# Dense attention on one Trainium2 core: value products of two key tiles in one go, with four sets of probabilities

## The chip, the cores and the metric

The kernel is one program on one core of a Trainium2 chip. The metric is the device time of a whole execution in microseconds (us); of several runs the median is given.

## What is computed

The reference is a chain of eight blocks on x of 2 x 512 rows of 256: four attentions, each followed by a feed-forward block. Two parts of it are plain softmax attentions of 16 heads of 16, and these two are what the change is about:

```
# part 6 of the program ("l3"): x attends to a context of 1024 rows, per batch
logit = jnp.einsum('bhnd,bhmd->bhnm', q, k)          # q already scaled
attn  = jax.nn.softmax(logit, axis=-1)
out   = jnp.einsum('bhnm,bhmd->bhnd', attn, v)

# part 5 ("m2"): x attends to its own 512 rows
scores = jnp.einsum('bqhd,bkhd->bhqk', q, k) * scale
probs  = jax.nn.softmax(scores, axis=-1)
out    = jnp.einsum('bhqk,bkhd->bqhd', probs, v)
```

All other blocks are left as they are.

## The kernel before, in words

`dense_attention` (from line 803) is called once for m2, with 512 keys, and once for l3, with 1024. It works through G = 8 groups (2 batches x 4 groups of heads) of S = 4 heads each, with 512 queries. The keys of a group are cut into tiles of 128: NC_ = 4 tiles in m2, 8 in l3. Each group needs two passes over the scores:

- **First pass** (`first_pair`, matmul at L893): queries on the partitions, keys along the free axis, two banks of PSUM (1024 scores a row) at a time. VectorE reduces such a pair to row maxima (`row_maxima`, L976, tile `shift`). There are two such pairs of banks, and pair k is written only after pair k-2 has been reduced (semaphore `pair_used`). The maxima of a group are transposed (`turn`, L900), negated and cut into two parts by VectorE (`cut`, L985 and L987), and put by two DMAs (L853) into two rows of the augmented queries `qa`, so that the second scores come out already shifted. A group has 8 pairs in m2 and 16 in l3.
- **Second pass** (`second`, L909): keys on the partitions, one matmul for each head of a tile, in three PSUM banks used in turn (semaphore `exp_done`: matmul i waits for exponential i-3). ScalarE takes the exponential (L1037) into `probs` in SBUF. `value_products(n, t)` (L919) then multiplies the probabilities of tile t of group n by the values: four matmuls, one for each head, on four column strips of 32 of the array, accumulated over the tiles in one bank (VALUES). They are float32, and the trace shows each as two records. A column "of v" holds a one, so that the denominators come out with them. Behind the last tile ScalarE copies the bank to `o_all` (L1040).

TensorE's order is written out by hand at the end of the tensor block. For each tile it is: pair, two seconds, pair, two seconds; behind them, from the second tile of a group, the value products of the tile before. First pairs run ahead of the second pass by one group and LEAD = 4 pairs (EARLY), so in tile t of group n the first pairs are of group n+1 and, from t = 2 in m2 (t = 6 in l3), of group n+2; the last 6 tiles of m2 and the last 10 of l3 have none left. `turn(n + 1)` stands behind the scores of tile NC_ - 2.

The operands of a group come through three buffers (BUFS). SyncE issues `load_qk(n - 1 + BUFS)`, four DMAs at L664 and L667, and `load_v` (L673) when the value products of group n-1 are done (`pv_done`). GpSimd clears two rows of the same buffer (L874) at the same point. `first_pair` with k = 0 waits for these loads (`qk_loaded`).

In the last group, `denominators` (L930) and `spread_pair` (L940) are put between the tiles; VectorE makes the reciprocals for them.

Of the kernel before, what the change touches and what calls it, by code (L numbers as in the profile page):

```python
# [9 lines left out]
ACT = mybir.ActivationFunctionType  # L10
AX = mybir.AxisListType

P = 128
# [3 lines left out]
NQ = 512  # L17
# [785 lines left out]
def dense_attention(nc, name, ps, ident, slot_pick, spread, nk, tiles, o_all):  # L803


    G, S, BUFS, LOADS = 8, 4, tiles.BUFS, tiles.LOADS
    NC_ = nk // P
# [11 lines left out]
    def pair_place(i):  # L819

        return i + max(0, (i - 2) // PAIRS)

    def turn_place(n):

        return (n + 1) * PAIRS + 2 + n if n < G - 1 else ALL + n

    LAST = ALL + G
    with Stage(nc, name) as s:
# [1 line left out]
        qk_loaded, v_loaded = tiles.qk_loaded, tiles.v_loaded  # L830
        shift = s.sb("shift", [P, 2, ROWS])
        minus_hi, minus_lo = s.sb("minus_hi", [ROWS, P], F32R), s.sb("minus_lo", [ROWS, P], F32R)
        probs = s.sb("probs", [P, 2 * S, NQ])
        rden = s.sb("rden", [P, NQ])
        rden_parts = s.sb("rden_parts", [P, NQ], F32R)
        zeroed = s.sem("zeroed")
# [3 lines left out]
        scored, exp_done, pv_done = s.sem("scored"), s.sem("exp_done"), s.sem("pv_done")  # L840
# [5 lines left out]
        @block.sync  # L846
        def _(sp):
            def place(n):
                sp.wait_ge(lo_ready, n + 1)
                if n >= BUFS:  # L850
                    sp.wait_ge(shift_cleared, n - BUFS + 1)
                for part, src in enumerate((minus_hi, minus_lo)):
                    sp.dma_start(qa[64 + part:65 + part, n % BUFS, :, :].rearrange("o h (t n) -> o (h t) n", n=P  # L853
                                                                                   ).bitcast(F32),
                                 src[:, :].bitcast(F32)).then_inc(shift_placed, 16)

            tiles.finish_first(sp)
            place(0)
            for n in range(G - 1):
                if n > 0:  # L860
                    sp.wait_ge(pv_done, NC_ * n)
                    if n - 1 + BUFS < G:
                        tiles.load_qk(sp, n - 1 + BUFS)
                    tiles.load_v(sp, n + 1)
                place(n + 1)
# [10 lines left out]
        @block.tensor  # L876
        def _(pe):
            def first_pair(i):
                n, k = divmod(i, PAIRS)
                buf = n % BUFS  # L880
                if k == 0:
                    pe.wait_ge(qk_loaded[buf], LOADS * (n // BUFS + 1))
                    if n < BUFS:
                        pe.wait_ge(filled, 2 * n + 2)
                    else:
                        pe.wait_ge(shift_cleared, n - BUFS + 1)
                at = pair_place(i)
                if at >= 2:
                    pe.wait_ge(pair_used, at - 1)
                for half in range(2):  # L890
                    r, j = divmod(2 * k + half, NH)
                    h, t = divmod(r, QT)
                    ins = nc.tensor.matmul(ps[:, 2 * (at % 2) + half, :], qa[:, buf, h, t * P:(t + 1) * P],  # L893
                                           ka[:, buf, h, j * BANK:(j + 1) * BANK], start=True, stop=True)
                ins.then_inc(pair_made, 1)

            def turn(n):
                at = turn_place(n)
                pe.wait_ge(pair_used, max(at - 1, pair_place((n + 1) * PAIRS - 1) + 1))
                nc.tensor.transpose(ps[0:ROWS, 2 * (at % 2), 0:P], shift[:, n % 2, :], ident[:, :]  # L900
                                    ).then_inc(shift_turned, 1)

            def second(n, t, h):
                i, buf = (n * NC_ + t) * S + h, n % BUFS
                if t == 0 and h == 0:
                    pe.wait_ge(shift_placed, 32 * n + 32)
                if i >= 3:
                    pe.wait_ge(exp_done, i - 2)
                nc.tensor.matmul(ps[:, 4 + i % 3, :], ka[:, buf, h, t * P:(t + 1) * P], qa[:, buf, h, :],  # L909
                                 start=True, stop=True).then_inc(scored, 1)  # L910

            def value_products(n, t):
                pe.wait_ge(exp_done, (n * NC_ + t) * S + S)
                if t == 0:
                    pe.wait_ge(v_loaded[n % 2], 16 * (n // 2 + 1))
                if t == 0 and n > 0:
                    pe.wait_ge(o_copied, n)
                for h in range(S):
                    ins = nc.tensor.matmul(ps[32 * h:32 * h + 32, VALUES, :], v[:, n % 2, t, h, :],  # L919
                                           probs[:, t % 2 * S + h, :], start=(t == 0), stop=(t == NC_ - 1))  # L920
                ins.then_inc(pv_done, 1)

            def denominators(half):
                begin, end = HALVES[half]
                m, at = 4 * (end - begin), LAST + 4 * half
                pe.wait_ge(o_copied, end)
                pe.wait_ge(pair_used, at - 1)
                for n in range(begin, end):
                    pick = 28 - 4 * (n - begin)
                    ins = nc.tensor.matmul(ps[64:64 + m, 2 * (at % 2), :], slot_pick[:, pick:pick + m], o_all[:, n, :],  # L930
                                           start=(n == begin), stop=(n == end - 1))
                ins.then_inc(den_made, 1)

            def spread_pair(i):
                half = 0 if i < 3 else 1
                at = LAST + 1 + half + i
                pe.wait_ge(rden_lo, half + 1)
                pe.wait_ge(pair_used, at - 1)
                for j in range(2):
                    ins = nc.tensor.matmul(ps[:, 2 * (at % 2) + j, :], spread[64:128, 2 * i + j - HALVES[half][0], :],  # L940
                                           rden_parts[64:128, :], start=True, stop=True)
                ins.then_inc(pair_made, 1)

            for i in range(PAIRS + 2):
                first_pair(i)
            turn(0)
            for i in range(PAIRS + 2, EARLY):
                first_pair(i)
            for n in range(G):
                for t in range(NC_):  # L950
                    for h in range(S):
                        i = EARLY + 2 * (n * NC_ + t) + h // 2
                        if h % 2 == 0 and i < ALL:
                            first_pair(i)
                        second(n, t, h)
                    if t == TURN_AT and n < G - 1:
                        turn(n + 1)
                    if n == G - 1 and t == 0:
                        denominators(0)
                    if n == G - 1 and 1 <= t <= 3:  # L960
                        spread_pair(t - 1)
                    if t > 0:
                        value_products(n, t - 1)
                value_products(n, NC_ - 1)
            denominators(1)
            spread_pair(3)
# [61 lines left out]
        @block.scalar  # L1028
        def _(act):
            for n in range(G):  # L1030
                for t in range(NC_):
                    for h in range(S):
                        i = (n * NC_ + t) * S + h
                        act.wait_ge(scored, i + 1)
                        if i >= 2 * S:
                            act.wait_ge(pv_done, n * NC_ + t - 1)
                        nc.scalar.activation(probs[:, t % 2 * S + h, :], ps[:, 4 + i % 3, :], ACT.Exp  # L1037
                                             ).then_inc(exp_done, 1)
                act.wait_ge(pv_done, n * NC_ + NC_)
                nc.scalar.activation(o_all[:, n, :], ps[:, VALUES, :], ACT.Copy).then_inc(o_copied, 1)  # L1040
# [1990 lines left out]
```

## Time and profile before

| | |
|---|---|
| time, median of 3 runs | 3491.04 us (3489.39 to 3491.08) |
| the profiled execution's own time | 3486.16 us |
| its span | 3484.4 us |
| TensorE busy in the span | 2558.5 us (73%) |
| VectorE busy | 2113.5 us (61%) |
| ScalarE busy | 1431.6 us (41%) |
| mean granted TensorE clock | 0.845 of full speed |
| second pass of m2, from the first L909 to the last | 2506.1 to 2631.0 us |
| second pass of l3, the same | 3029.2 to 3233.4 us |

"Busy" is the share of the span in which an engine has a computing instruction in flight. A matmul's record lasts longer than the time it keeps the next one from starting, so the distance of two starts tells more than a duration. The two attentions of the change take about a tenth of the span together. A timeline merges like instructions that follow each other: "0.73 PE L893 ... x2" is two matmuls, from the start of the first to the end of the last.

### The profile page before, as it was taken

What the parts mean: (1) busy time and instruction counts of PE and PEld (TensorE: products, weight loads), DVE (VectorE), ACT (ScalarE), POOL (GpSimd) and SP (SyncE); (2) the same over time, 40 slices, a digit from 0 to 9 for tenths busy, and PEclk for the clock granted to TensorE, in tenths of its full rate; (3) what the DMA queues carried; (4) which work ended last, traced back from release to release, by engine and by line L of the source; (5) the groups of instructions that cost most, each with busy time, mean ns of one, the idle gap of its engine ahead of it and who ended that gap; (6) DMA issues with size and microseconds to landing.
All of it is one profiled execution on the core that took longest, in us unless ns stands there. A gap on an engine that the chain in (4) does not pass through costs nothing. (4 is left out here: it accounts for less than half of the span.)

```text
span 3484.4 us, 37704 instructions
## 1 busy us (share of the span) xinstructions
PE 2558.5 (73%) x12065; PEld 1618.6 (46%) x12066; DVE 2113.5 (61%) x4913; ACT 1431.6 (41%) x2245; POOL 423.8 (12%) x228
## 2 busy tenths in 40 slices
PE   2999999536366666665499459788785896899598
PEld 1444444324233333333499435455443775454387
DVE  4667666575777777753366435665654565676377
ACT  1444444111677887773244122221251231266221
POOL 0000000002000000000477302111100211100021
PEclk8999999767677777776699779999797997899799
DMA  1000000206011111000366200000420110631010
GB/s 57 14 14 9 14 14 0 87 5 209 9 25 25 25 25 25 7 1 8 120 205 201 79 28 1 0 0 0 141 65 23 42 42 14 187 89 41 29 41 30
DMA packets 72294, 170.09 MB, mean 49 GB/s; under 512 B 10185, under 2 KB 38865, under 8 KB 68689
## 3 DMA queue, kind: packets, MB, share of 16 engines
q1 hardware_dynamic: 70608, 164.11, 15.9%
q0 software_dynamic: 1536, 4.20, 0.4%
q8 instruction: 68, 1.11, 0.1%
q14 instruction: 82, 0.66, 0.1%
HBM read 129.09 MB, written 38.80 MB: 48 GB/s over the span
## 5 line engine op out<-in xcount | busy, mean ns | idle before, releaser
L1449 ACT ACTIVATE l1a_over_s<-l1a_sc_s,l1a_minus_step_s 128x1024 bf16<-128x1024 f32 x256 | 290.0, 1139 | 3.5 <-DVE l1a_minus_step_s L1323 2.2
L1263 DVE MAX8 l1a_cand_s<-ps 128x8 f32<-128x128 f32 x1024 | 213.2, 284 | 70.5 <-PE ps L1158 67.2
L1191 PE MATMUL ps<-l1a_probs_s,l1h_v_s 128*32 128x256 f32 x1024 | 124.3, 574 | 158.6 <-ACT l1a_probs_s L1457 157.4
L1435 ACT ACTIVATE l1a_sc_s<-ps,l1a_minus_tau_s 128x1024 f32<-128x1024 f32 x128 | 141.9, 1112 | 139.6 <-DVE l1a_minus_tau_s L1292 53.4
L976 DVE TENSOR_REDUCE l3a_shift_s<-ps 128x1 f32<-128x1024 f32 x128 | 150.2, 1219 | 50.6 <-PE ps L893 50.6
L538 DVE TENSOR_SCALAR l0a_probs_s<-l0a_probs_s 128x1024 f32<-128x1024 f32 x128 | 88.5, 691 | 150.5 <-ACT l0a_probs_s L605 150.0
L605 ACT ACTIVATE l0a_probs_s<-ps 128x1024 f32<-128x1024 f32 x128 | 131.1, 1024 | 104.5 <-PE ps L455 103.3
L1158 PE MATMUL ps<-l1h_ka_s,l1h_qa_s 128*128 128x512 f32 x256 | 132.0, 559 | 56.3 <-DVE l1a_cand_s L1263 46.2
L1037 ACT ACTIVATE l3a_probs_s<-ps 128x512 f32<-128x512 f32 x256 | 132.8, 603 | 87.0 <-PE ps L909 86.7
L1914 PE MATMUL ps<-m1e_x_part_s,m1e_up_part_s 128*128 128x256 f32 x1152 | 151.9, 290 | 13.9 <-POOL m1e_up_part_s L2094 12.3
L1914 PEld LDWEIGHTS ps<-m1e_x_part_s,m1e_up_part_s 128*128 128x128 f32 x1152 | 144.6, 196 | 17.3 <-POOL m1e_up_part_s L2094 15.4
L1457 ACT ACTIVATE l1a_probs_s<-ps 128x1024 f32<-128x1024 f32 x128 | 125.7, 1016 | 62.3 <-PE ps L1179 62.3
L1179 PEld LDWEIGHTS ps<-l1h_qa_s,l1h_ka_s 128*128 128x128 f32 x512 | 96.6, 262 | 98.2 <-issue 63.5
L1179 PE MATMUL ps<-l1h_qa_s,l1h_ka_s 128*128 128x256 f32 x512 | 128.4, 390 | 17.1 <-ACT l1a_sc_s L1435 12.9
L466 PE MATMUL ps<-l0a_probs_s,l0a_v_s 128*64 128x512 f32 x512 | 138.0, 617 | 0.3 <-ACT l0a_den_s L613 0.3
L469 PE MATMUL ps<-l0a_probs_s,ones 128*64 128x512 f32 x512 | 131.6, 592 | 0.0
L455 PE MATMUL ps<-l0a_q_hi_s,l0a_k_parts_s 128*128 128x512 f32 x256 | 122.5, 479 | 2.6 <-PE ps L439 0.3
L1168 PE MATMUL ps<-l1h_ka_s,l1h_qa_s 128*128 128x512 f32 x256 | 100.2, 501 | 29.7 <-ACT l1a_sc_s L1435 29.7
L1191 PEld LDWEIGHTS ps<-l1a_probs_s,l1h_v_s 128*32 128x32 f32 x1024 | 24.7, 134 | 206.0 <-ACT l1a_probs_s L1457 181.0
L1700 PE MATMUL ps<-m3e_x_part_s,m3e_up_part_s 128*128 128x512 f32 x432 | 101.9, 397 | 21.9 <-DVE m3e_x_part_s L1762 18.2
L2563 PE MATMUL ps<-g_qu_part_s,g_k 128*128 128x512 f32 x288 | 97.9, 481 | 26.4 <-DVE g_qu_part_s L2677 26.1
L2094 POOL TENSOR_TENSOR m1e_up_part_s<-m1e_up_s,m1e_up_part_s 128x1536 fp32r<-128x1536 f32 x30 | 105.1, 3505 | 69.4 <-ACT m1e_up_part_s L1948 69.4
(574 smaller groups left out, 5698.9 us busy)
## 6 DMA issues: line engine op xcount, KB each, us to landing
m1e_up_s<-m_up SPq DMA_DIRECT2D x32, 768.0 KB, 4.3
m1e_down_s<-m_down SPq DMA_DIRECT2D x16, 768.0 KB, 4.4
l1h_ka_s<-l_k_parts SPq DMA_DIRECT2D x16, 512.0 KB, 8.0
l3h_ka_s<-l_k_parts SPq DMA_DIRECT2D x16, 512.0 KB, 7.9
l0a_w_s<-l_w SPq DMA_DIRECT2D x16, 384.0 KB, 3.0
m3ew_up_s<-m_up SPq DMA_DIRECT2D x6, 768.0 KB, 4.3
m_sorted<-ones SPq DMA_DIRECT2D x1, 4096.0 KB, 16.6
l1h_qa_s<-l_q_parts SPq DMA_DIRECT2D x16, 256.0 KB, 6.1
```

The lines of the kernel that those rows point to most:

```text
L466: nc.tensor.matmul(ps[64 * h:64 * h + 64, 6, :], v[:, p, t, 64 * h:64 * h + 64], probs[:, t % SLOTS, h * NQ:(h + 1) * NQ], start=(t == 0), ...
L469: ins = nc.tensor.matmul(ps[64 * h:64 * h + 64, 7, :], ones[:, 0:64], probs[:, t % SLOTS, h * NQ:(h + 1) * NQ], start=(t == 0), stop=(t == ...
L605: nc.scalar.activation(probs[:, t % SLOTS, :], ps[:, 2 * (t % 2):2 * (t % 2) + 2, :].rearrange("p a n -> p (a n)"), ACT.Exp).then_inc(exp_ ...
L976: nc.vector.reduce_max(shift[:, n % 2, rows * k:rows * k + rows], ps[:, 2 * (at % 2):2 * (at % 2) + 2, :].rearrange("p (r j) n -> p r (j n ...
L1037: nc.scalar.activation(probs[:, t % 2 * S + h, :], ps[:, 4 + i % 3, :], ACT.Exp).then_inc(exp_done, 1)
L1158: nc.tensor.matmul(ps[:, A0 + f % 2, :], qa[:, buf, h, at:at + P], ka[:, buf, h, j * BANK:(j + 1) * BANK], start=True, stop=True).then_inc ...
L1179: ins = nc.tensor.matmul(ps[:, PAIR + 2 * (place % 2) + h // 2, h % 2 * HALF:h % 2 * HALF + HALF], ka[:, buf, h, t * P:(t + 1) * P], qa[:, ...
L1191: ins = nc.tensor.matmul(ps[32 * h:32 * h + 32, VALUES, 0:HALF], v[:, n % 2, t, h, :], probs[:, t % 4, h * HALF:(h + 1) * HALF], start=(t ...
L1263: ins = nc.vector.max(cand[:, r, 8 * (c + j * 4):8 * (c + j * 4) + 8], ps[:, A0 + f % 2, c * P:(c + 1) * P])
L1435: nc.scalar.activation(sc[:, r, :], ps[:, PAIR + 2 * (place % 2):PAIR + 2 * (place % 2) + 2, :].rearrange("p a n -> p (a n)"), ACT.Relu, b ...
L1449: nc.scalar.activation(over[:, done % 2, :], sc[:, r, :], ACT.Relu, bias=minus_step[:, r:r + 1], accum_out=total[:, i, r:r + 1]).then_inc( ...
L1914: ins = nc.tensor.matmul(ps[:, u % 4, way * TOK:(way + 1) * TOK], up_parts[a][:, b % 2, k, way, c, :], x_parts[p][:, b % 2, k, :], start=( ...
```

## The change

`probs` holds four sets (of four heads) in place of two. The value products of tiles t-2 and t-1 are issued together behind the scores of every even tile t > 0, and those of the last two tiles together behind the last tile. ScalarE's wait for a free set moves accordingly: it waits for the value products of four tiles back.

```diff
-        probs = s.sb("probs", [P, 2 * S, NQ])
+        probs = s.sb("probs", [P, 4 * S, NQ])
...
                     ins = nc.tensor.matmul(ps[32 * h:32 * h + 32, VALUES, :], v[:, n % 2, t, h, :],
-                                           probs[:, t % 2 * S + h, :], start=(t == 0), stop=(t == NC_ - 1))
+                                           probs[:, t % 4 * S + h, :], start=(t == 0), stop=(t == NC_ - 1))
...
-                    if t > 0:
+                    if t > 0 and t % 2 == 0:
+                        value_products(n, t - 2)
                         value_products(n, t - 1)
+                value_products(n, NC_ - 2)
                 value_products(n, NC_ - 1)
...
-                        if i >= 2 * S:
-                            act.wait_ge(pv_done, n * NC_ + t - 1)
-                        nc.scalar.activation(probs[:, t % 2 * S + h, :], ps[:, 4 + i % 3, :], ACT.Exp
+                        if i >= 4 * S:
+                            act.wait_ge(pv_done, n * NC_ + t - 3)
+                        nc.scalar.activation(probs[:, t % 4 * S + h, :], ps[:, 4 + i % 3, :], ACT.Exp
```

How this moves TensorE's instructions, first in l3: the second and the third tile (t = 1 and 2) of a group in the middle. L893 are first pairs (into the banks that VectorE reduces), L909 the second scores, L919 the value products. Before:

```order
L893 MATMUL ps<-l3h_ka_s,l3h_qa_s 128x512 x2
L909 MATMUL ps<-l3h_qa_s,l3h_ka_s 128x512 x2
L893 MATMUL ps<-l3h_ka_s,l3h_qa_s 128x512 x2
L909 MATMUL ps<-l3h_qa_s,l3h_ka_s 128x512 x2
L919 MATMUL ps<-l3a_probs_s,l3h_v_s 32x512 x4
L893 MATMUL ps<-l3h_ka_s,l3h_qa_s 128x512 x2
L909 MATMUL ps<-l3h_qa_s,l3h_ka_s 128x512 x2
L893 MATMUL ps<-l3h_ka_s,l3h_qa_s 128x512 x2
L909 MATMUL ps<-l3h_qa_s,l3h_ka_s 128x512 x2
L919 MATMUL ps<-l3a_probs_s,l3h_v_s 32x512 x4
```

and with the change:

```order
L893 MATMUL ps<-l3h_ka_s,l3h_qa_s 128x512 x2
L909 MATMUL ps<-l3h_qa_s,l3h_ka_s 128x512 x2
L893 MATMUL ps<-l3h_ka_s,l3h_qa_s 128x512 x2
L909 MATMUL ps<-l3h_qa_s,l3h_ka_s 128x512 x2
L893 MATMUL ps<-l3h_ka_s,l3h_qa_s 128x512 x2
L909 MATMUL ps<-l3h_qa_s,l3h_ka_s 128x512 x2
L893 MATMUL ps<-l3h_ka_s,l3h_qa_s 128x512 x2
L909 MATMUL ps<-l3h_qa_s,l3h_ka_s 128x512 x2
L919 MATMUL ps<-l3a_probs_s,l3h_v_s 32x512 x8
```

The value products of tile 0 have moved behind the scores of tile 2, so that with tile 0's own scores three tiles of scores stand in a row at the head of a group.

Second, the same place in m2, where tile 2 holds the first pairs of the group after next, and the turn (L900, which transposes the maxima `m2a_shift_s`). Before:

```order
L893 MATMUL ps<-m2h_ka_s,m2h_qa_s 128x512 x2
L909 MATMUL ps<-m2h_qa_s,m2h_ka_s 128x512 x2
L893 MATMUL ps<-m2h_ka_s,m2h_qa_s 128x512 x2
L909 MATMUL ps<-m2h_qa_s,m2h_ka_s 128x512 x2
L919 MATMUL ps<-m2a_probs_s,m2h_v_s 32x512 x4
L893 MATMUL ps<-m2h_ka_s,m2h_qa_s 128x512 x2
L909 MATMUL ps<-m2h_qa_s,m2h_ka_s 128x512 x2
L893 MATMUL ps<-m2h_ka_s,m2h_qa_s 128x512 x2
L909 MATMUL ps<-m2h_qa_s,m2h_ka_s 128x512 x2
L900 MATMUL ps<-ident,m2a_shift_s 16x128
L919 MATMUL ps<-m2a_probs_s,m2h_v_s 32x512 x4
```

and with the change:

```order
L893 MATMUL ps<-m2h_ka_s,m2h_qa_s 128x512 x2
L909 MATMUL ps<-m2h_qa_s,m2h_ka_s 128x512 x2
L893 MATMUL ps<-m2h_ka_s,m2h_qa_s 128x512 x2
L909 MATMUL ps<-m2h_qa_s,m2h_ka_s 128x512 x2
L893 MATMUL ps<-m2h_ka_s,m2h_qa_s 128x512 x2
L909 MATMUL ps<-m2h_qa_s,m2h_ka_s 128x512 x2
L893 MATMUL ps<-m2h_ka_s,m2h_qa_s 128x512 x2
L909 MATMUL ps<-m2h_qa_s,m2h_ka_s 128x512 x2
L900 MATMUL ps<-ident,m2a_shift_s 16x128
L919 MATMUL ps<-m2a_probs_s,m2h_v_s 32x512 x8
```

The value products of tile 0, which stood ahead of the third L893 row of this piece, now stand behind the turn.

## Rows read from the trace of the kernel before

**Rows 1.** The page, part 1: busy us of each engine (share of the span), instructions.
```profile
PE 2558.5 (73%) x12065; PEld 1618.6 (46%) x12066; DVE 2113.5 (61%) x4913; ACT 1431.6 (41%) x2245; POOL 423.8 (12%) x228
```
**Rows 2.** Windows of two l3 groups: us, each engine's busy us (instructions), granted clock, DMA.
```profile
3079.12:3104.10 24.98, 24.98 (x134) 12.65 (x130) 19.22 (x18) 17.21 (x33) 1.80 (x1) 1.00 0.38 86
3104.10:3129.10 25.00, 25.00 (x134) 12.65 (x130) 19.22 (x18) 17.21 (x33) 1.80 (x1) 1.00 0.38 86
```
**Rows 3.** Timeline of an l3 group's start: start, us, engine, line, instructions [idle before, releaser].
```profile
3102.07 2.10 PE L919 MATMUL ps<-l3a_probs_s,l3h_v_s 128*32 128x512 f32 x16
3104.10 0.73 PE L893 MATMUL ps<-l3h_ka_s,l3h_qa_s 128*128 128x512 f32 x2
3104.87 4.62 DVE L976 TENSOR_REDUCE l3a_shift_s<-ps 128x1 f32<-128x1024 f32 x4 [1.76 <-PE ps L893]
3105.10 4.28 ACT L1037 ACTIVATE l3a_probs_s<-ps 128x512 f32<-128x512 f32 x8 [0.26 <-PE ps L909]
3106.15 0.30 PEld L893 LDWEIGHTS ps<-l3h_ka_s,l3h_qa_s 128*128 128x128 f32 x2 [0.21 <-DVE l3a_shift_s L976]
3107.28 0.30 PEld L893 LDWEIGHTS ps<-l3h_ka_s,l3h_qa_s 128*128 128x128 f32 x2 [0.37 <-DVE l3a_shift_s L976]
3108.43 1.06 PE L919 MATMUL ps<-l3a_probs_s,l3h_v_s 128*32 128x512 f32 x8
3109.42 0.72 PE L893 MATMUL ps<-l3h_ka_s,l3h_qa_s 128*128 128x512 f32 x2
3109.99 0.63 PE L909 MATMUL ps<-l3h_qa_s,l3h_ka_s 128*128 128x512 f32 x2
3110.45 0.62 PE L893 MATMUL ps<-l3h_ka_s,l3h_qa_s 128*128 128x512 f32 x2
3111.50 1.06 PE L919 MATMUL ps<-l3a_probs_s,l3h_v_s 128*32 128x512 f32 x8
```
**Rows 4.** Timeline of the end of l3's seventh group, where first pairs run out.
```profile
3193.59 0.73 PE L893 MATMUL ps<-l3h_ka_s,l3h_qa_s 128*128 128x512 f32 x2
3195.68 1.06 PE L919 MATMUL ps<-l3a_probs_s,l3h_v_s 128*32 128x512 f32 x8
3196.68 0.96 PE L909 MATMUL ps<-l3h_qa_s,l3h_ka_s 128*128 128x512 f32 x3
3197.21 2.07 ACT L1037 ACTIVATE l3a_probs_s<-ps 128x512 f32<-128x512 f32 x4 [0.55 <-PE ps L909]
3198.40 1.06 PE L919 MATMUL ps<-l3a_probs_s,l3h_v_s 128*32 128x512 f32 x8
```
**Rows 5.** Waits in m2, 2518 to 2600 us: total us, times, longest.
```profile
PE ps L893 <- DMA m2h_ka_s<-m_k_parts: 10.9, 5, 2.3
```
**Rows 6.** Windows of m2's second to sixth group, columns as in rows 2.
```profile
2518.93:2533.91 14.98, 12.77 (x70) 6.34 (x66) 9.79 (x10) 8.95 (x17) 1.80 (x1) 1.00 0.40 89
2533.91:2550.13 16.22, 14.18 (x69) 6.56 (x65) 9.79 (x10) 9.06 (x17) 1.80 (x1) 0.89 0.36 83
2550.13:2565.13 15.00, 12.74 (x70) 6.33 (x66) 9.79 (x10) 8.95 (x17) 1.80 (x1) 1.00 0.40 89
2565.13:2581.61 16.48, 14.15 (x70) 7.08 (x66) 9.89 (x10) 9.05 (x17) 1.80 (x1) 0.90 0.37 82
2581.61:2597.87 16.26, 14.18 (x69) 6.58 (x65) 9.79 (x10) 9.06 (x17) 1.80 (x1) 0.90 0.36 82
```
**Rows 7.** Timeline of m2's third group: its start, the wait, and what follows.
```profile
2538.21 1.07 PE L919 MATMUL ps<-m2a_probs_s,m2h_v_s 128*32 128x512 f32 x8
2541.32 0.73 PE L893 MATMUL ps<-m2h_ka_s,m2h_qa_s 128*128 128x512 f32 x2 [2.04 <-DMA m2h_ka_s<-m_k_parts]
2544.09 1.94 PE L919 MATMUL ps<-m2a_probs_s,m2h_v_s 128*32 128x512 f32 x8
```
**Rows 8.** Timeline, last group of l3, behind its longest idle time.
```profile
3214.81 0.97 PE L940 MATMUL ps<-l3a_rden_parts_s,spread 64*128 64x512 f32 x2 [3.11 <-DVE l3a_rden_parts_s L1003]
3215.71 1.93 PE L919 MATMUL ps<-l3a_probs_s,l3h_v_s 128*32 128x512 f32 x8
```

## The prediction

> **What bounds the kernel now.** I read the page first, to see that TensorE is the busiest engine but with a quarter of the span unused, VectorE next [rows 1]; that says nothing of the two attentions by themselves. So I cut l3 into its groups by windows: in the middle a group takes 24.98 to 25.00 us and TensorE is busy for all of it, while VectorE is busy 19.22 and ScalarE 17.21 [rows 2]. The time there is the length of TensorE's own sequence, and whatever stretches it counts in full. The timeline of one such group then shows what the sequence is made of [rows 3]. I call a run of scores between two sets of value products a stretch, and measure from start to start:
>
> - one tile of scores: 3109.42 to 3111.50, 2.08 us;
> - value products of one tile: 3108.43 to 3109.42, 0.99; of two tiles in a row, at the end of a group: 3102.07 to 3104.10, 2.03;
> - two tiles of scores in a row, at the start of a group: 3104.10 to 3108.43, 4.33.
>
> Six single tiles, one stretch of two, six single value products, one double one, and 0.20 for the turn make 12.48 + 4.33 + 5.94 + 2.03 + 0.20 = 24.98, the window's time, so nothing is left over.
>
> The stretch of two holds the point of the case: it takes 4.33, not 2 x 2.08 = 4.16, though one entry and one exit less stand in it. Its third and fourth pair waited for VectorE [rows 3]: four reductions took 4.62 us, 1.13 apart with the last one 1.23 long, and a pair is written only once the pair two before it is reduced. Scores of a tile ask VectorE for two reductions, 2.3 us, and keep TensorE 2.08. With single tiles VectorE catches up during the value products; in a longer stretch it cannot.
>
> For m2 the waits show another limit: five times, 10.9 us in all, TensorE waits for the keys of the group after next [rows 5]. That is at tile 2, right behind the value products of tile 0: they started at 2538.21 and took 0.99, then 2.04 us idle until 2541.32 [rows 7]. The loads leave when the group before has ended (2533.91), so their landing is fixed to a group's start, some 7.4 us behind it, whatever TensorE does meanwhile.
>
> **The change, part by part.** It adds and removes no instruction on any engine; it moves value products. Per group the stretches of l3 were 2, 1, 1, 1, 1, 1, 1 tiles and become 3, 2, 2, 1; in m2 2, 1, 1 become 3, 1. 24 alternations go in l3 and 8 in m2.
>
> *l3, first six groups.* Value products: before 6 x 0.99 + 2.03 = 7.97, now 4 x 2.03 = 8.12, **+0.15**. The two stretches of two tiles start as the measured one does, behind a double value product with VectorE and both pairs of banks free: 2 x (4.33 - 4.16) = **+0.34**. The stretch of three goes on at VectorE's pace, two more pairs at 1.13: 4.33 + 2.26 = 6.59, against 4.33 + 2.08 before, **+0.18**. ScalarE is not behind: eight exponentials took 4.28 us in the stretch of 4.33 [rows 3], and its two exponentials for each pair, 1.07 at that rate, fit into the pair's 1.13. Sum +0.67 a group, **+4.0** in six.
>
> *l3, seventh group.* Without first pairs a tile's scores are limited by the three banks: the fourth second waits for the first exponential. Before, from the first second at 3196.68 to the value products at 3198.40 is 1.72 us with the turn, and the tile ahead of it took 2.09, 3.81 together [rows 4]. Joined to the tile ahead of it, its four seconds wait for the exponentials one by one. They come about 0.49 apart (four in 2.07 us [rows 4], one of them about 0.6, the 2.07 less 0.6 over three). The first exponential begins some 0.5 us behind its second, so 1.0 after the stretch begins, and ends at 1.6; the last second needs the fifth one, at 1.6 + 4 x 0.49 = 3.6, and the value products come near 4.2 with the turn, against 3.8 before: +0.4. With the other stretches as above (+0.18, +0.17) and the value products (+0.15) it is **+0.9**. The last group has one such joined stretch (+0.4) and two places where an alternation less is pure gain (-0.2 each): 0.
>
> *m2, second to sixth group.* The value products of tile 0 ran before the load's landing, in time that TensorE would have waited. Now they come behind it and the idle time grows from about 2.2 to 3.2 us. The group ends later by what was hidden, 0.99, and by 0.05 for 2.03 + 2.03 against 0.99 + 0.99 + 2.03. VectorE is idle at that point, so nothing else moves: 5 x 1.04 = **+5.2**. I keep the load's own time, since its DMAs are the same and leave at the same point of the group. If part of the wait went (say the loads landed 1 us earlier), this term would be near 0; nothing earlier in the queue changes, so I take the full one.
>
> *m2, the clock.* Of these five groups two ran in 14.98 and 15.00 us with a granted clock of 1.00, three in 16.22, 16.48 and 16.26 at 0.89 to 0.90 [rows 6]: behind an idle time of 2.04 us the next value products lasted 1.94 us [rows 7] instead of 1.06 [rows 3], which is the 1.2 GHz level. One such drop costs 16.32 - 14.99 = 1.33 us. Behind 3.11 us of idle time the clock was low in l3's last group as well [rows 8]. With the idle time at 3.2 us I expect all five to drop: two more, **+2.7**. Bounds: none more, 0 (even -4.0 if none of the five dropped, which longer idling doesn't suggest); and five that each cost what rows 8 suggest (the products 0.9 longer, the scores behind them as much again by estimate, 1.8 in all), 9.0 - 4.0 = +5.0.
>
> The Trainium skill, "TensorE: Matmul & The Clock Gate" (Part 1, HAM oscillation), says that the array runs at half rate unless activity keeps it up, and describes a loop in which every wait for a DMA brings it back down. By that rule all five groups drop, +2.7; the trace so far agrees in three of five.
>
> *m2, the rest.* First group: stretch of three +0.18, products +0.05, +0.2. Seventh, where first pairs end behind tile 1: joined scores, +0.4. Eighth: 0, since it is taken up with denominators and waits that stand at the same places.
>
> *What costs nothing.* ScalarE's wait now asks for value products four tiles back, which always stand a whole stretch earlier. The turn, the cut and the two DMAs of the maxima get about 1 us more before the next group's first second. The larger `probs` moves no data. GpSimd's clearing hangs on the same event as before.
>
> **Sum**: 4.0 + 0.9 + 5.2 + 2.7 + 0.2 + 0.4 = **+13.4 us**. Against the profiled execution (3486.16) that is 3499.6; its own time lies 4.9 under the median of the runs, so against the median it is 3504.4. A measurement of this kernel can tell about 0.2%, 7 us, from no change.
>
> **A rule that speaks the other way.** One round of a two-tile stretch without waits can be read off rows 3: a tile's four couples of matmuls cost 2.08 with entry and exit, one inside a stretch 0.46 (3109.99 to 3110.45), so entry and exit cost about 0.24 together; a merged value product gives back 0.05 of it. An alternation less is thus worth 0.2 us where nothing waits. The Trainium skill, "TensorEngine Tiling (Array Packing)", Key Properties, has the rule behind it: "Changing tiling mode (not just tile) drains the TensorE". The value products use four column strips and the scores the whole array, so by that rule the change is a plain gain.
>
> **Rivals.**
>
> 1. *Faster: the drains count and the waits don't arise.* In this case VectorE's pace would not bind, and the stretch of two that already exists would lose its 0.41 of waits too; the middle groups of l3 would take 5.76 + 2 x 3.92 + 2.08 + 0.20 + 8.12 = 24.0, 1.0 less each, 7 in all with the seventh, and m2 0.2 less in each group, 1.4: 3491.0 - 8.4 = **3482.6**. Against it: the two waits of 0.21 and 0.37 stand in the trace at just the place that becomes the rule. It decides if VectorE's reductions came less than 1.0 apart; they are at 1.13. The chance is 0.06.
> 2. *Only l3 loses.* The value products of tile 0 in m2 cost nothing because the load lands about 1 us sooner than before, or the clock drops less for it: 3491.0 + 5 = **3496**. For it: the five waits are not all alike (2.04 and up to 2.3). Against it: not by 1 us, and the two groups at full clock agree to 0.02 [rows 6]. 0.14.
> 3. *The clock costs more.* Each of the five waits of 3.2 us drops the clock for as long as in rows 8, or longer: +5.0 and up to twice that in place of +2.7, **3507 to 3512**. For it: the one idle time of 3.11. Against it: the three groups that dropped lost 1.33 on average, since TensorE is busy right behind the wait. 0.16.
> 4. *No effect at all*: **3491**, 0.03. TensorE's order does change as the listing shows, so this needs all terms to cancel.
>
> The forecast itself, 3501 to 3507 with the clock's bounds, has 0.61.
>
> **The numbers.** Slower by over 0.2% (above 3498) are the forecast and rival 3: 0.77. Within 0.2% are rivals 2 and 4: 0.17. Faster: 0.06. The time is that of the forecast, 3504. The range runs from rival 2 (3496) to within rival 3 (3511), which leaves out rivals 1 and 4 and the ends of 3.
>
> **What would show it.** In l3, windows of middle groups near 25.65 us, with value products only as x16, three waits of L893 for L976 more in the stretch of three and two in each of two. In m2, idle times of L893 before the keys of 3.2 us, no value products between the group's start and it, windows of 17.3 us, and a granted clock under 1.00 in all five. The prediction is wrong if l3's groups stay at or under 25.0 (VectorE's pace does not bind), or if m2's waits keep 2.2 us (the landing is not tied to the group's start).

## The result, and the profile after

The changed kernel took 3501.31 us in the median (3497.87 to 3503.51, 6 runs) against 3490.84 before (3488.63 to 3492.95, 6 runs): a ratio of 1.003, 95% interval [1.0017, 1.0043]. That is 10.5 us more; 13.4 were forecast. The profiled execution took 3498.89.

The page of the changed kernel, part 1:

```profile
span 3497.1 us, 37688 instructions
...
PE 2567.3 (73%) x12065; PEld 1626.7 (47%) x12066; DVE 2110.7 (60%) x4913; ACT 1434.0 (41%) x2245; POOL 423.9 (12%) x228
```

As many computing instructions on each engine as before [rows 1]; only the time between them has changed. The windows of m2's second to sixth group, which answer to [rows 6]:

```profile
2518.74:2537.10 18.36, 15.13 (x70) 7.72 (x66) 9.88 (x10) 9.06 (x17) 1.80 (x1) 0.81 0.33 72
2537.10:2554.28 17.18, 14.09 (x70) 6.88 (x66) 9.88 (x10) 9.04 (x17) 1.80 (x1) 0.90 0.34 78
2554.28:2571.70 17.42, 14.04 (x70) 7.11 (x66) 9.89 (x10) 9.06 (x17) 1.80 (x1) 0.90 0.34 77
2571.70:2589.60 17.90, 14.00 (x70) 7.54 (x66) 9.89 (x10) 9.06 (x17) 1.80 (x1) 0.90 0.36 76
2589.60:2606.63 17.03, 14.04 (x70) 7.54 (x66) 9.88 (x10) 9.06 (x17) 1.80 (x1) 0.90 0.34 78
```

The five take 87.89 us where they took 78.94, and the granted clock is under 1.00 in all of them, not in three. The waits in the same stretch, answering to [rows 5], and the timeline of the third group, answering to [rows 7]:

```profile
PE ps L893 <- DMA m2h_ka_s<-m_k_parts: 16.6, 5, 3.9
```

```profile
2544.56 0.73 PE L893 MATMUL ps<-m2h_ka_s,m2h_qa_s 128*128 128x512 f32 x2 [3.09 <-DMA m2h_ka_s<-m_k_parts]
2547.53 2.69 PE L919 MATMUL ps<-m2a_probs_s,m2h_v_s 128*32 128x512 f32 x16
```

The keys land 7.46 us behind the group's start at 2537.10 (7.41 in the third group before, counted from 2533.91), but no value products stand ahead of the wait any more. In l3, two of the five windows of middle groups, which answer to [rows 2]:

```profile
3063.65:3088.70 25.05, 25.05 (x134) 12.72 (x130) 18.93 (x18) 17.50 (x33) 1.80 (x1) 1.00 0.36 85
3088.70:3113.78 25.08, 25.08 (x133) 12.73 (x129) 18.93 (x18) 17.52 (x33) 1.80 (x1) 1.00 0.36 85
```

The other three are 25.03 to 25.10. That is 0.07 over the group before, not 0.67, and only just above the 25.0 at which the prediction called itself wrong. The timeline of the first of them, TensorE, answering to [rows 3], shows where the forecast went off:

```profile
3061.62 2.10 PE L919 MATMUL ps<-l3a_probs_s,l3h_v_s 128*32 128x512 f32 x16
3063.65 0.73 PE L893 MATMUL ps<-l3h_ka_s,l3h_qa_s 128*128 128x512 f32 x2
...
3070.21 1.92 PE L919 MATMUL ps<-l3a_probs_s,l3h_v_s 128*32 128x512 f32 x16
3072.07 0.72 PE L893 MATMUL ps<-l3h_ka_s,l3h_qa_s 128*128 128x512 f32 x2
...
3076.37 1.92 PE L919 MATMUL ps<-l3a_probs_s,l3h_v_s 128*32 128x512 f32 x16
3078.22 0.72 PE L893 MATMUL ps<-l3h_ka_s,l3h_qa_s 128*128 128x512 f32 x2
...
3082.73 1.92 PE L919 MATMUL ps<-l3a_probs_s,l3h_v_s 128*32 128x512 f32 x16
3084.59 0.73 PE L893 MATMUL ps<-l3h_ka_s,l3h_qa_s 128*128 128x512 f32 x2
...
3086.66 2.11 PE L919 MATMUL ps<-l3a_probs_s,l3h_v_s 128*32 128x512 f32 x16
```

The stretches are 6.56 (3063.65 to 3070.21), 4.30, 4.51 with the turn, and 2.07 us, as worked out from the rows before (6.59, 4.33, 4.53, 2.08). In the stretch of three each pair from the third on waits for a reduction, here the fifth:

```profile
3067.95 0.30 PEld L893 LDWEIGHTS ps<-l3h_ka_s,l3h_qa_s 128*128 128x128 f32 x2 [0.36 <-DVE l3a_shift_s L978]
```

But a double value product in the middle of a group takes 1.86, 1.85 and 1.86 us, and only the one at a group's end 2.03. The weight loads of the two kinds differ:

```profile
3062.65 0.16 PEld L919 LDWEIGHTS ps<-l3a_probs_s,l3h_v_s 128*32 128x32 f32 x8 [0.88 <-ACT l3a_probs_s L1039]
...
3070.67 0.13 PEld L919 LDWEIGHTS ps<-l3a_probs_s,l3h_v_s 128*32 128x32 f32 x4 [0.30 <-issue]
3071.10 0.13 PEld L919 LDWEIGHTS ps<-l3a_probs_s,l3h_v_s 128*32 128x32 f32 x4 [0.30 <-issue]
```

At a group's end the second tile's weights come 1.03 us behind the first's (3061.62 to 3062.65), held by ScalarE's last exponentials. In the middle the four-strip rounds follow each other 0.43 apart without a gap: two tiles are four rounds, 1.72, and one entry of 0.13 (a round is the four heads' matmuls in one of their two records; the entry is what a set of value products takes beyond its rounds). The value before of 2.03 held such a wait.

### The profile page after: what moved, and what is told of

Same layout as the page of the kernel before. It is cut to its first block and busy times, and to the rows that moved or that the text cites. A ratio compares the mean times of both kernels' runs of the same rounds, so it can differ in the third digit from the quotient of the medians.

```text
span 3497.1 us, 37688 instructions
## 1 busy us (share of the span) xinstructions
PE 2567.3 (73%) x12065; PEld 1626.7 (47%) x12066; DVE 2110.7 (60%) x4913; ACT 1434.0 (41%) x2245; POOL 423.9 (12%) x228
```

## The experiments

The theory after the result (A): m2 loses because tile 0's value products no longer fill the wait for the keys, and the longer wait brings the clock down each time; l3 is about even, because what the merged products give back, the scores lose to VectorE's pace. Its rivals: (B) the merging itself, or the clock alone, makes the loss; (C) the landing of the keys isn't tied to the issue. Each run was timed next to the kernel before, and the ratios below are to it.

**The two attentions apart.** `l3_only` and `m2_only` keep the merged order in one of them:

```diff
-                    if t > 0 and t % 2 == 0:
-                        value_products(n, t - 2)
-                        value_products(n, t - 1)
-                value_products(n, NC_ - 2)
+                    if nk == 1024:          # nk == 512 in m2_only
+                        if t > 0 and t % 2 == 0:
+                            value_products(n, t - 2)
+                            value_products(n, t - 1)
+                    elif t > 0:
+                        value_products(n, t - 1)
+                if nk == 1024:
+                    value_products(n, NC_ - 2)
                 value_products(n, NC_ - 1)
```

> The merged order only in the attention with 1024 keys (l3); the one with 512 keys (m2) issues its value products tile by tile as before. Theory A (m2 loses because the value products of tile 0 no longer fill the wait for the keys; l3 is near even because longer stretches of scores wait for VectorE and the merged value products give the same back): m2 windows back to 15.0 to 16.5 us, l3 windows 25.0 to 25.1, last l3 group about 1 us longer; time 3491 + 2 = 3493. Rival B (merging itself costs in both places by the stretches): 3496.

> The merged order only in m2, l3 as before. Theory A: all five waits for the keys near 3.2 us, clock low behind each, m2 8 us longer than before, l3 windows 24.98 to 25.00: 3499. Rival B: half of the loss, 3496.

Measured: `l3_only` 3492.76 us, ratio 1.0003 [0.9994, 1.0012]; `m2_only` 3498.97, ratio 1.0020 [1.0011, 1.0029]. The waits of m2, first of `l3_only`, then of `m2_only`:

```profile
PE ps L893 <- DMA m2h_ka_s<-m_k_parts: 11.6, 5, 2.7
```

```profile
PE ps L893 <- DMA m2h_ka_s<-m_k_parts: 16.4, 5, 3.4
```

The second to sixth group of m2 together, in the same order:

```profile
2522.92:2602.58 79.66, 68.05 (x329) 33.07 (x326) 49.17 (x50) 45.06 (x85) 9.01 (x5) 0.94 0.38 84
2520.68:2608.55 87.87, 71.50 (x329) 36.40 (x325) 49.44 (x50) 45.29 (x85) 9.01 (x5) 0.88 0.34 76
```

With m2's order left alone the five groups take 79.66 us (78.94 in the kernel before), with m2 merged 87.87 (87.89 in the changed kernel). Both came out where theory A had them. The time of `m2_only` alone would still allow rival B's 3496, since its interval reaches down to 3495; its windows don't. The loss that a measurement can tell lies in m2; l3 alone can't be told from no change. Even its 0.07 us a group is uncertain: from one copy to `o_all` to the next, l3's middle groups in the old order took 25.00 to 25.05 us in `m2_only`, against 24.98 to 25.00 in the kernel before.

**The loads issued earlier.** The queries and keys of a group are read by scores alone, so their buffer is free when its second scores are done; the value products, for which the loads waited, don't touch it. `early_old` is the kernel before and `early_new` the changed one, both with:

```diff
-                    sp.wait_ge(pv_done, NC_ * n)
+                    sp.wait_ge(scored, NC_ * S * n)
                     if n - 1 + BUFS < G:
                         tiles.load_qk(sp, n - 1 + BUFS)
+                    sp.wait_ge(pv_done, NC_ * n)
                     tiles.load_v(sp, n + 1)
...
-                pool.wait_ge(pv_done, NC_ * (n + 1))
+                pool.wait_ge(scored, NC_ * S * (n + 1))
```

> The kernel before, but the loads of queries and keys (and GpSimd's clearing of the two rows) wait for the second scores of the group (semaphore scored) in place of its value products, which read neither. Theory A (the landing is tied to the moment of issue): the loads leave about 2.0 us earlier, the five waits fall from 2.2 to about 0.2 us, the clock stays up, groups of 12.9 us: 10 us and 4 us of clock less, 3477. Rival C (the loads are limited by the DMA queues' other traffic and land when they did): waits stay at 2 us, 3491.

> The changed kernel with the same earlier issue of the loads. Theory A: waits fall from 3.3 to about 1.2 us, so 10 us less; the clock drops in some of the five at most, 3 to 6 us less: 3487 to 3490, still 10 above the old order with early loads, since 1 us of value products a group is uncovered as long as any wait is left. Rival B (the loss of m2 lies in the clock alone): as soon as the clock stays up it equals the old order with early loads to within 3 us.

Measured: `early_old` **3475.22 us**, ratio 0.9958 [0.9945, 0.9972]; `early_new` 3481.56, ratio 0.9974 [0.9965, 0.9983]. Waits and windows of m2's second to sixth group, `early_old` (its L894 is L893 of before):

```profile
PE ps L894 <- DMA m2h_ka_s<-m_k_parts: 1.3, 4, 0.6
```

```profile
2520.61:2533.51 12.90, 12.76 (x70) 6.34 (x66) 9.80 (x10) 8.96 (x17) 1.80 (x1) 1.00 0.45 98
2533.51:2546.55 13.04, 12.72 (x70) 6.32 (x66) 9.79 (x10) 8.95 (x17) 1.80 (x1) 1.00 0.48 105
2546.55:2559.87 13.32, 12.75 (x70) 6.34 (x66) 9.79 (x10) 8.95 (x17) 1.80 (x1) 1.00 0.47 98
2559.87:2572.81 12.94, 12.74 (x70) 6.33 (x66) 9.79 (x10) 8.96 (x17) 1.80 (x1) 1.00 0.47 104
2572.81:2585.79 12.98, 12.74 (x70) 6.33 (x66) 9.80 (x10) 8.96 (x17) 0.00 (x0) 1.00 0.41 92
```

and `early_new`:

```profile
PE ps L894 <- DMA m2h_ka_s<-m_k_parts: 6.3, 5, 1.6
```

```profile
2516.40:2530.10 13.70, 12.59 (x70) 6.43 (x66) 9.79 (x10) 8.95 (x17) 1.80 (x1) 1.00 0.42 96
2530.10:2545.71 15.61, 14.03 (x70) 7.23 (x66) 9.89 (x10) 9.05 (x17) 1.80 (x1) 0.89 0.39 86
2545.71:2559.53 13.82, 12.58 (x70) 6.44 (x66) 9.80 (x10) 8.95 (x17) 1.80 (x1) 1.00 0.44 97
2559.53:2573.35 13.82, 12.61 (x70) 6.44 (x66) 9.79 (x10) 8.95 (x17) 1.80 (x1) 1.00 0.43 97
2573.35:2587.13 13.78, 12.61 (x70) 6.43 (x66) 9.79 (x10) 8.95 (x17) 0.00 (x0) 1.00 0.39 87
```

The first load of a group leaves so much sooner, in the kernel before (the group starts at 2533.91) and in `early_old` (2533.51):

```profile
2534.04 0.57 SPq L664 DMA_DIRECT2D m2h_qa_s<-m_q_parts  x1
```

```profile
2531.57 0.57 SPq L664 DMA_DIRECT2D m2h_qa_s<-m_q_parts  x1
```

This settles two things. The landing is tied to the issue: loads that leave 2.1 us sooner (0.13 us behind the group's start, now 1.94 ahead of it) take about 2 us out of each wait, so C falls. And the loss in m2 isn't the clock alone: of these ten groups nine ran at the full clock, and at that clock the merged order is still 0.7 us a group slower (13.78 in the mean of four against 13.04 of five). Worked out from the pieces it is the uncovered 0.99 less the 0.13 that a merged product saves, 0.86; the landings differ by a few tenths from group to group. The one group at 0.89, whose wait was the longest with 1.58 us, cost 1.8 us more, 0.4 of it in the wait itself. I had expected `early_new` at 3487 to 3490. It came at 3481.56, 20 us under the changed kernel, where my own terms (10 for the waits, 3 to 6 for the clock) make 13 to 16. The five groups gave 17.2 of it (70.73 us against 87.89): 10.3 in the waits and some 7 in the clock, which stayed up in four of five groups behind waits of 1.1 to 1.2 us. The rest isn't traced.

`early_old` beats both kernels: 16 us under the one before in the median (5 runs). `early_new` is 6 us behind it, more than the 3 that rival B allowed.

**Place without merging.** `lag_two` has four sets of probabilities and the later place, but one tile at a time:

```diff
-                    if t > 0 and t % 2 == 0:
+                    if t > 1:
                         value_products(n, t - 2)
-                        value_products(n, t - 1)
                 value_products(n, NC_ - 2)
                 value_products(n, NC_ - 1)
```

> The changed kernel without the merging: four sets of probabilities, but the value products of tile t-2 behind tile t, one tile at a time (three tiles in a row only at a group's end). This moves tile 0's value products behind the wait for the keys as the change does, and merges nothing. Theory A (place, not merging, makes m2's loss): waits for the keys near 3.2 us and m2 about 8 us longer, as in the changed kernel; time 3498 to 3501. Rival (the merged block itself, or what it does to the clock, makes the loss): m2 as in the kernel before, 3491 to 3493. In l3 the three value products in a row at a group's end should take 1.85 + 1.04 = 2.9 us if only the last one waits for its exponentials.

Measured: 3496.52 us, ratio 1.0021 [1.0012, 1.0030]. m2's waits and its second to sixth group:

```profile
PE ps L893 <- DMA m2h_ka_s<-m_k_parts: 16.1, 5, 3.5
```

```profile
2522.19:2540.41 18.22, 15.11 (x70) 7.84 (x66) 9.88 (x10) 9.05 (x17) 1.80 (x1) 0.81 0.32 73
2540.41:2555.96 15.55, 12.42 (x70) 6.53 (x66) 9.79 (x10) 8.96 (x17) 1.80 (x1) 1.00 0.38 86
2555.96:2572.76 16.80, 13.76 (x70) 7.61 (x66) 9.89 (x10) 9.05 (x17) 1.80 (x1) 0.90 0.35 80
2572.76:2589.78 17.02, 13.79 (x70) 7.66 (x66) 9.89 (x10) 9.06 (x17) 1.80 (x1) 0.90 0.36 79
2589.78:2607.00 17.22, 13.67 (x70) 7.58 (x66) 9.89 (x10) 9.05 (x17) 1.80 (x1) 0.90 0.35 77
```

The waits are as long as in the changed kernel, and the five groups take 84.81 us, 5.87 more than before, with nothing merged ahead of the group's end. So the place, with the clock that falls behind the longer waits, makes most of m2's loss. The time is 1.5 us under the range I gave, and the groups 3 us under the changed kernel's 87.89. Part of that is the second of them, which kept its clock (15.55 us at 1.00) behind a wait of 3.13 us: the drop isn't certain. In l3 the three value products in a row took 2.71 us, not 2.9:

```profile
3058.62 2.78 PE L919 MATMUL ps<-l3a_probs_s,l3h_v_s 128*32 128x512 f32 x24
```

and the next scores start at 3061.33. Six rounds of 0.43 and one entry of 0.13 are 2.71: behind two tiles of products the exponentials of the last one are ready, so that nothing waits. Its middle groups in l3 took 24.83 to 24.86 us (from one copy to `o_all` to the next), 0.15 under those of the kernel before.

**VectorE's pace.** `half_old` and `half_new` are the two orders with a reduction over half of each pair, so that the row maxima are those of half the keys:

```diff
-                                     ps[:, 2 * (at % 2):2 * (at % 2) + 2, :].rearrange("p (r j) n -> p r (j n)", r=rows),
+                                     ps[:, 2 * (at % 2):2 * (at % 2) + rows, 0:512 // rows],
```

> The kernel before, with VectorE reducing half of each pair's scores (512 of 1024, so the maxima are of half the keys), everything else in place. VectorE's reduction falls from 1.22 to about 0.65 us and its pace no longer binds. Theory A: in l3 only the one stretch of two tiles of a group gains, 0.4 us: windows of 24.6 us.

> The changed kernel with the same half reductions. Theory A (VectorE's pace eats the gain of the merged order in l3): the stretches of two and three tiles lose their waits for VectorE, 0.4 us each and 0.8 in the stretch of three, unless ScalarE's exponentials (0.49 apart through three banks) become the next limit; windows of 23.5 to 24.2 us, 0.4 to 1.1 under those of the old order with half reductions. Rival (VectorE doesn't bind, the merged stretches are long for another reason, the array's own changes of mode): windows stay at 25.0, above the old order.

Measured: 3477.67 us (ratio 0.9964 [0.9952, 0.9976]) and 3480.89 (0.9977 [0.9967, 0.9987]). Two l3 groups of `half_old`, then two of `half_new`:

```profile
3048.02:3072.68 24.66, 24.66 (x133) 12.59 (x129) 11.54 (x18) 17.01 (x33) 1.80 (x1) 1.00 0.39 86
3072.68:3097.32 24.64, 24.64 (x133) 12.59 (x130) 11.54 (x18) 17.01 (x33) 1.80 (x1) 1.00 0.38 87
```

```profile
3052.69:3076.56 23.87, 23.87 (x133) 12.68 (x130) 11.56 (x18) 16.70 (x33) 1.80 (x1) 1.00 0.38 89
3076.56:3100.42 23.86, 23.86 (x133) 12.67 (x129) 11.55 (x18) 16.70 (x33) 1.80 (x1) 1.00 0.39 90
```

With VectorE out of the way (11.5 us busy for 18.9 to 19.2) the merged order is 0.8 us a group *faster* than the old one; with it in the way, 0.07 slower. The old order gains 0.34 by the shorter reductions, the merged one 1.2. So the merging has a value, and VectorE's pace through two pairs of banks is what takes it away. In `half_new` the stretch of three took 6.00 us (3076.56 to 3082.56 in its timeline), not the 5.76 of a stretch without waits. ScalarE, through its three banks, is the next limit; its twelve exponentials of that stretch run without a gap:

```profile
3077.56 5.99 ACT L1039 ACTIVATE l3a_probs_s<-ps 128x512 f32<-128x512 f32 x12 [0.26 <-PE ps L909]
```

About half of the 13 us that `half_old` gains on the kernel before lies at the head of l3: from l3's first pair to its first copy to `o_all`, where first pairs have little else beside them, it took 46.0 us, against 52.7 in the kernel before. The whole program isn't faster with the merged order even so, since m2 loses as before (its waits are 17.9 us, 12.8 in `half_old`).

## Why the prediction was right, point by point

- **m2, uncovered value products (+5.2).** Right in mechanism and nearly in size. The waits grew from 10.9 to 16.6 us, by 5.7, of which 5.0 were forecast; the landings varied more than I took (7.46 us behind the start in one group, 8.26 in another). The merged products took 0.13 off each group where I had added 0.05, so the term is 5 x 0.86 = 4.3 and 0.7 for the landings. Shown by `m2_only`, by `lag_two` (place without merging) and by the full-clock groups of `early_new`.
- **m2, the clock (+2.7).** Right in direction, all five groups dropped, but mis-sized. At the full clock a group would take 14.98 + 0.86 = 15.84; the five took 8.7 us more than five times that, 0.7 of it in waits above the forecast, so 1.6 for each drop in place of 1.33. Less the 4.0 that three drops cost before, that is about +4.0 (an estimate from these windows) in place of +2.7. The dearest drop was the second group's, 18.36 us at 0.81. The whole of the five groups was forecast at +7.9 and is +8.95. That all five would drop was partly luck: `lag_two`, with the same waits, kept one up, and in the kernel before the length of the wait didn't order them (last section).
- **l3, value products (+0.15 a group).** The term that failed. I took the double value product at 2.03 us from the only place where the kernel before has one [rows 3], the end of a group. There the second half waits for the last exponentials. Without that wait it is 1.85: 3 x 1.85 + 2.03 = 7.58 in place of 8.12, or -0.39 against before in place of +0.15. It accounts for nearly all that l3's middle groups were off by (+0.07 measured, +0.67 forecast).
- **l3, stretches of scores (+0.52 a group).** Right: each stretch within 0.03 us of what was worked out, and the cause, VectorE's pace, shown by the waits for its reductions and by `half_new` against `half_old`.
- **l3 in all.** From its first pair to its output projection's first matmul (timelines: 3001.59 to 3249.74, now 3010.98 to 3261.10) it took 2.0 us more, 4.9 were forecast. The first six groups gave +0.5 where +4.0 was forecast, the seventh +0.3 for +0.9, the last, from copy to copy, +1.2 for 0. That last one is merged order and clock mixed: it took 32.84 us before and 34.06 after, 34.12 in `l3_only` and 34.03 in `early_new`, but 35.13 in `early_old`, which has the old order; the granted clock there was 0.95, 0.90, 0.90, 0.90 and 0.85. So its +1.2 isn't shown to come from the order.
- **The rule on changes of mode.** "Changing tiling mode (not just tile) drains the TensorE" (the Trainium skill, "TensorEngine Tiling (Array Packing)", Key Properties): the runs agree in sign. An entry into the value products costs 0.13 us, and once the waits for VectorE are short, the merged order gains 0.8 a group. With the full reductions the waits for VectorE take that gain back. That the 0.13 is the drain itself no run here shows.
- **Rivals.** The second (only l3 loses) fell with `l3_only`, the first (waits for VectorE don't arise) with the timelines. The third (more clock) was right in kind, and in size the clock's part came out between the two, about 4.0 against 2.7 in the forecast and 5.0 or more in the rival; the rival's time, 3507 to 3512, didn't come. *No effect* falls with the interval, which begins at 1.0017.

From its first pair to its output projection's first matmul, m2 took 7.8 us more in the profiles and l3 2.0, together +9.7 where 13.4 were forecast. The direction and most of the size came from m2. Nearly all of the difference is l3's first six groups. The other terms were off too and cancel by luck: in m2 the five groups came 1.05 above the forecast, and the last group, from copy to copy, gave 1.2 back where 0 was forecast, with a granted clock of 0.85 for 0.79. The two profiled executions differ by 12.7 us and the medians by 10.5, so some 3 us of the profiled difference lie outside the two attentions, where the programs are the same.

## What to carry to other kernels

A block that stands ahead of a wait for a DMA is free time filled; before moving it, look which wait it stands ahead of. Grouping like work on TensorE paid here only as far as the engines that empty its banks kept pace: a run of scores longer than the banks hold gave the gain back. And look at a transfer's issue before you move work around its wait: ask which instruction last reads the buffer, and wait for that one alone, which here was worth more than either order of the matmuls.

## What the runs showed that I had not expected

- A merged value product is cheaper than the kernel before could show: rounds of four strips follow 0.43 us apart, with 0.13 for the first entry, whether four or six rounds follow (1.85 and 2.71 us).
- The clock fell in one group of `early_new` behind a wait of 1.58 us and stayed at 1.00 in one of `lag_two` behind 3.13. In the kernel before it fell behind waits of 2.04, 2.08 and 2.33 us and stayed up behind 2.21 and 2.26. So how long TensorE idles doesn't by itself tell which group will drop; what does is open here. The Trainium skill ("TensorE: Matmul & The Clock Gate", Part 1, HAM oscillation) describes a loop in which every wait for a DMA, 3 to 5 us long there, brings the clock down. Of the waits of about 3 us and more the changed kernel agrees in five of five groups and `lag_two` in four; about shorter ones, as in `early_new`, that loop says nothing.
